# Deformable convolution after attention on one core: three of nine taps sampled densely instead of two

## The reference

```python
offset_feat = conv2d(concat([feat_l, feat_up * 2]), W_off, pad=0)          # 1x1
om = conv2d(offset_feat, W_om, pad=1) + b_om                              # 3x3 -> offsets and mask
feat_align = relu(deform_conv_v2(feat_up, offset, sigmoid(mask), W_dcn, b_dcn))
return feat_align + feat_l
```

## Time and profile before

| | before |
|---|---|
| median of 3 runs | 12687.91 us (12680.93 to 12688.98) |
| the profiled execution's own time | 12682.99 us |
| its span, first to last instruction | 12681.2 us |
| PE busy / weight loads | 9257.2 us (73%) / 5057.7 us (40%) |
| DVE busy | 7291.4 us (57%) |
| ACT busy | 4747.5 us (37%) |
| POOL busy | 10320.1 us (81%) |
| mean granted TensorE clock | 0.838 |

### The profile page before, as it was taken

The page is one execution under the profiler, slowest core; times in us unless marked ns, Lnnn a source line. Parts: engine busy times, 40 slices in busy tenths (PEclk is TensorE's granted clock), DMA queues, the critical chain, the costliest instruction groups (busy, mean ns, idle before and its releaser), DMA issues. The chain is left out here.

```text
span 12681.2 us, 168047 instructions
## 1 busy us (share of the span) xinstructions
PE 9257.2 (73%) x56052; PEld 5057.7 (40%) x56052; DVE 7291.4 (57%) x10291; ACT 4747.5 (37%) x6104; POOL 10320.1 (81%) x21509
## 2 busy tenths in 40 slices
PE   4677778775778777776577777777577777777754
PEld 1244444442444444443244344444234444444444
DVE  4356566644666666664566666665456666666443
ACT  1344444432434434433244344343233434334322
POOL 0278888885788888888488888888858888888888
PEclk7888888886888888888788888888788888888876
DMA  1222211110011111111011111111101111111100
GB/s 48 77 67 70 66 23 24 24 24 23 21 33 25 24 24 25 25 24 29 13 25 33 24 24 25 25 23 24 28 16 31 25 25 25 25 23 24 24 22 21
DMA packets 373774, 373.51 MB, mean 29 GB/s; under 512 B 129440, under 2 KB 219936, under 8 KB 372768
## 3 DMA queue, kind: packets, MB, share of 16 engines
q0 software_dynamic: 229376, 235.34, 8.9%
q10 hardware_dynamic: 97920, 71.35, 1.8%
q1 hardware_dynamic: 45472, 54.53, 1.6%
HBM read 316.66 MB, written 44.04 MB: 28 GB/s over the span
## 5 line engine op out<-in xcount | busy, mean ns | idle before, releaser
L469 POOL DMA_INDIRECT g<-patches,idx x7168 | 7156.6, 998 | 1112.4 <-issue 949.5
L905 DVE TENSOR_REDUCE mx<-ring 128x2 f32<-128x1024 f32 x2048 | 2411.1, 1220 | 2919.3 <-PE ring L666 2381.8
L541 ACT ACTIVATE p<-ring 128x1024 f32<-128x1024 f32 x2048 | 1984.8, 1021 | 3832.3 <-PE ring L724 2960.3
L465 POOL TENSOR_TENSOR carrier<-carrier 128x1 f32<-128x1 f32 x13824 | 3063.5, 250 | 122.0
L708 PE MATMUL ps_x<-fx,hats 128*128 128x208 f32 x12288 | 2520.1, 356 | 120.4 <-DVE hats L1048 78.8
L721 PE MATMUL ring<-qf,kf 32*128 32x512 f32 x8192 | 1459.9, 786 | 1515.3 <-ACT hats L551 816.3
L708 PEld LDWEIGHTS ps_x<-fx,hats 128*128 128x128 f32 x12288 | 2192.2, 196 | 671.2 <-issue 598.1
L734 PE MATMUL ps_a<-p,v 128*64 128x512 f32 x4096 | 1442.3, 790 | 39.0 <-DVE shared L932 37.6
L734 PE MATMUL ps_b<-p,v 128*64 128x512 f32 x4096 | 1247.2, 692 | 0.0
L1067 DVE TENSOR_TENSOR ps_x<-ps_x,chosen 128x416 f32<-128x416 f32 x1024 | 611.1, 597 | 1053.2 <-PE ps_x L708 844.1
L574 ACT COPY vt<-ps_x 128x256 f32<-128x256 f32 (+1 forms) x512 | 204.5, 399 | 2659.1 <-PE ps_x L780 1505.9
(11 more groups left out here) (125 smaller groups left out, 7601.4 us busy)
## 6 DMA issues: line engine op xcount, KB each, us to landing
g<-patches,idx POOLq DMA_INDIRECT x7168
patch_in<-in_fpad ACTq DMA_DIRECT2D x544, 64.0 KB
patches<-patch_out ACTq DMA_DIRECT2D x136, 256.0 KB
fx<-in_fpad SPq DMA_DIRECT2D x20, 416.0 KB
p<-in_x SPq DMA_DIRECT2D x4, 2048.0 KB
xq<-in_x SPq DMA_DIRECT2D x32, 256.0 KB
fs_s<-in_fs SPq DMA_DIRECT2D x32, 256.0 KB
xs<-in_x SPq DMA_DIRECT2D x32, 256.0 KB
```

Source lines behind the costliest of these rows:

```text
L465: last = nc.gpsimd.tensor_tensor(carrier[:, col:col + 1], carrier[:, 0:1], carrier[:, 0:1], ALU.add)
L469: nc.gpsimd.indirect_dma_start(out=g[:, j, :], out_offset=None, in_=patches[b], in_offset=bass.IndirectOffsetOnAxis(ap=idx[:, t, j:j + 1], ...
L541: nc.scalar.activation(p[:, (2 * kt + pair) % 4, :, :], ring[slot][:, :, :], ACT.Exp, scale=SCALE)\
L905: V.tensor_reduce(mx[:, n:n + 2, c], ring[slot][:, :, :], AX.X, ALU.max).then_inc(ring_free[slot], 1)
```

## The change

`DENSE` goes from 2 to 3 and `PICKED` from 7 to 6. Everything else follows from that or makes it fit:

- a tile has 48 indirect gathers instead of 56, in parts of 2, 2, 1 and 1 taps instead of 2, 2, 2 and 1;
- a tile has 6 sets instead of 4, which begin at key tiles 0, 1, 2, 4, 5, 6 of its eight; where one set's half 1 and the next set's half 0 fall on the same key tile, half 1 comes first;
- `hats` has three buffers instead of two, and ACT cuts the hats straight after the distances, in the same key tile;
- dense tap 0 is turned with part 2 and dense taps 1 and 2 with part 3; `vt` is ordered by these slots, and `align` goes through them by a table.

```diff
-DENSE = 2
+DENSE = 3
 PICKED = TAPS - DENSE
 PARTS = 4
 CUTS = tuple(min(2 * part, PICKED - (PARTS - part)) for part in range(PARTS + 1))
-LAST_TAPS = CUTS[PARTS] - CUTS[PARTS - 1] + DENSE
+DENSE_CUTS = (0, 0, 0, 1, DENSE)
+WIDTHS = tuple(CUTS[part + 1] - CUTS[part] + DENSE_CUTS[part + 1] - DENSE_CUTS[part] for part in range(PARTS))
+SLOTS = tuple(sum(WIDTHS[:part]) for part in range(PARTS))
+SLOT_TAPS = tuple(tap for part in range(PARTS) for tap in (*range(CUTS[part], CUTS[part + 1]),
+                                                           *range(PICKED + DENSE_CUTS[part], PICKED + DENSE_CUTS[part + 1])))
+HATS = 3
...
-        hats = sb("hats", [128, 2, 1 + PAIRS, SET_GROUPS * 128])
+        hats = sb("hats", [128, HATS, 1 + PAIRS, SET_GROUPS * 128])
...
-            return tuple((r, t, i, half) for half in range(2) for r, t, i in sets_with(s, kt, half))
+            return tuple((r, t, i, half) for half in (1, 0) for r, t, i in sets_with(s, kt, half))
...
-                made = hats[:, i % 2, :, :]
+                made = hats[:, i % HATS, :, :]
...
-                    for r, t, i in weighed_at(s, kt):
-                        cut_hats(uses, t, i)
                     for r, t in aligned_at(s, kt):
                         finish_tile(tile_number(r, t))
...
                     for r, t, i in hats_at(s, kt):
                         distances_to_hats(uses, t, i)
+                        cut_hats(uses, t, i)
...
-                for tap in range(TAPS):
-                    last = mm(aligned, wdcn_s[:, tap, :], vt[:, tap, :], start=tap == 0, stop=tap == TAPS - 1)
+                for k, tap in enumerate(SLOT_TAPS):
+                    last = mm(aligned, wdcn_s[:, tap, :], vt[:, k, :], start=k == 0, stop=k == TAPS - 1)
...
-                if part == PARTS - 1:
-                    for d in range(DENSE):
-                        last = tr(turned[:, (picked + d) * 128:(picked + d + 1) * 128], dval[:, t % 2, d * C:(d + 1) * C],
-                                  ident_s[:, :])
+                for k, d in enumerate(range(DENSE_CUTS[part], DENSE_CUTS[part + 1]), picked):
+                    last = tr(turned[:, k * 128:(k + 1) * 128], dval[:, t % 2, d * C:(d + 1) * C], ident_s[:, :])
```

More of the change, by code:

```diff
@@ L325, in build @@
         assert all(slots_in(o) % 2 == 0 for o in (FIRST, MID, LAST))
-        assert MID[-1][0] == "rows" and MID[0][0] == ("scores", 0)
+        assert ("rows", 2) in MID and MID[0] == (("scores", 0), 2)
         BATCH_SLOTS = USES_KV + slots_in(FIRST) + (STEPS_B - 2) * slots_in(MID) + slots_in(LAST)
@@ L571, in keep_turned @@
                 m = part_number(r, t, part)
-                width = 128 * (LAST_TAPS if part == PARTS - 1 else CUTS[part + 1] - CUTS[part])
+                width = WIDTHS[part] * 128
                 act.wait_ge(val_turned, m + 1)
-                nc.scalar.copy(vt[:, CUTS[part]:CUTS[part] + width // 128, :].rearrange("p k n -> p (k n)"), turned[:, 0:width]).then_inc(vt_ready, 1)
+                nc.scalar.copy(vt[:, SLOTS[part]:SLOTS[part] + WIDTHS[part], :].rearrange("p k n -> p (k n)"), turned[:, 0:width]).then_inc(vt_ready, 1)
             def step(s, b, i):
@@ L707, in blocks_of_half @@
                     for pair in range(PAIRS):
-                        last = mm(cells, hats[:, i % 2, 1 + pair, j * 128:(j + 1) * 128], fx[:, pair, :, group * GC:(group + 1) * GC],
+                        last = mm(cells, hats[:, i % HATS, 1 + pair, j * 128:(j + 1) * 128], fx[:, pair, :, group * GC:(group + 1) * GC],
                                   start=pair == 0, stop=pair == PAIRS - 1)
```

## The result

The changed kernel takes 14784.01 us (median; 14776.14 to 14813.88), the kernel before beside it 12684.42 us. The ratio is 1.166, 95% interval 1.164 to 1.168: slower by a sixth. I had forecast 15290 us, a fifth slower; the measured time lies within the range, 14600 to 16000. The profiled execution has a span of 14775.8 us.

A forecast was written before the change was run, and what follows sets the result against it. POOL was taken as the bound, PE's loop close behind; middle steps of 350.3 + 105 us added dense work (39 + 34 + 28 + 5, less 1), summed with start, image-boundary steps and tail, gave about 15290 us, range 14600 to 16000.

The forecast's parts named there:

- the bound and its thinness: Middle steps: POOL never stops at 360.2 us a step, with PE's loop close behind at about 350.
- my signs: Expected: POOL waiting over 100 us a step for `val`, PE waiting at halves but not for `val`, middle steps 455 us.
- the distances: Eight added sets a step, each 1.23 us of PE's time plus 2.3 of waiting for ACT: 28 us.
- halves and their wait: Sixteen added halves a middle step on PE: 39 us of work plus 34 us of waiting for DVE.
- the new wait: PE waits for `half_used` between a key tile's two halves: 8 x 1.6 + 8 x 2.6 = 34 us a step.
- the floor: Middle step's period with POOL taken away, set by the loop of PE, ACT and DVE: about 350 us.
- a mean outside 0.83 to 0.90: PE's mean granted clock in middle steps, 0.87 before; leaving this range would show the prediction wrong.
- The case of a rising clock: Rival: added work fills idle time, PE's time at 1.2 GHz goes, at most 47 us a step; 13920 us, chance 0.2.
- the cut ahead of the exponentials: ACT comes 0.6 us late to the exponentials in 24 key tiles: 5 us a step, bounds 0 and 14.
- its check on the distances: Start: second step 332 against 375 and 379 us, 43 for two tiles; own terms give 28 for distances, 15 for others.
- The tail: End of the run, set by POOL: from 554 us to 430, bounds 385 and 554.
- The faster rival: Rival: PE has room, added work vanishes in its idle time and only POOL's time counts; 12120 us, chance 0.03.

The follow-up runs named there:

- experiment 1: Kernel before, without the seventh gathered tap's 8 gathers a tile (patches stay zero): 12012.03 us, ratio 0.948.
- experiment 5: Changed kernel with 8 more gathers a tile into a tile that nothing reads: 14871.48 us, ratio 1.173.
- experiment 4: Changed kernel with the halves of sets 1 and 4 left out on PE and DVE, their distances, hats and weighing kept: 12915.01 us, ratio 1.019.
- experiment 3: Changed kernel with the hats cut one key tile later, behind the exponentials, except at the last key tile: 14747.52 us, ratio 1.163.
- experiment 9: Kernel before with PE's half put behind the distances in key tiles that have distances: 12659.97 us, ratio 0.9975.
- experiment 2: Changed kernel with two dense taps and two hat buffers, so only the new order remains: 12722.02 us, ratio 1.004.
- experiment 10: Kernel before with PE's half behind the distances and one small POOL addition ahead of each gather instead of two: 12047.67 us, ratio 0.949.
- experiment 11: Kernel before with half behind distances, one POOL addition ahead of each gather, and the seventh tap's 8 gathers a tile left out: 14837.21 us, ratio 1.170.
- experiment 12: Kernel before, old order, with the seventh tap's 8 gathers a tile left out and one POOL addition ahead of each gather: 14503.09 us, ratio 1.141.
- experiment 6: Changed kernel without DVE's multiplication in every half: 14415.56 us, ratio 1.137.
- experiment 7: Changed kernel with PE's aligning, turning and distances moved between a key tile's first and second half: 13812.82 us, ratio 1.089.

## Why the prediction came out so

**Right: the bound and its thinness.** POOL was the bound and PE's loop stood right behind it (experiments 1 and 5). Of the 51 us that POOL saves a middle step, I gave the kernel 10. Without the added dense work it is 18. Of my signs, POOL's wait came as 127 us a step, but only half of it is for `val` and the rest for `idx`, which I had not named; PE's wait for `val` is gone, and DVE waits longer for PE at its maxima (413 us in four steps; before it was 299 and another 70 put down to issue).

**Right: the distances.** Experiment 4 against 1 holds the distances, the cut and the gathered tap that is no longer weighed: forecast 28 + 5 - 1 = 32 us a middle step, measured 28.4. PE's wait for ACT, the larger part of the distances, is (225.3 - 148.5) / 4 = 19 us a step more, where 8 x 2.3 = 18 was forecast.

**Right in kind, 10 us too large: halves and their wait.** Forecast 39 + 34, measured 62.6. The direct part holds: 16 x 2.47 = 39. The term that was mis-sized is the new wait. I took 1.6 us behind a normal key tile and 2.6 behind a sampling; the 64 waits are 1.6 us each on average, 25.6 a step. By place in the trace they are 1.4 us at key tiles 1 and 2, 1.6 at 5 and 2.0 at 6, so behind a sampling (2 and 6) 1.7 and not 2.6. That fits DVE being hardly late once PE itself is later by the added half, more than I allowed.

**Mis-sized: the floor.** I put PE's loop at 350 by taking away only PE's waits for `val`. It is 342.6, because PE's own instructions took less time at the higher clock. My sum left the clock's share as it was, and I had named a mean outside 0.83 to 0.90 as a sign of being wrong; it went from 0.87 to 0.91, in experiment 1 as in the changed kernel. The Trainium skill (TensorE: Matmul & The Clock Gate, What's actually happening) says that activity releases the throttle. Experiment 1 agrees with it, where PE's busy share of four steps rose from 78% to 79%. The changed kernel doesn't follow from it, since that share fell to 74% and the clock rose as much. The case of a rising clock, 13920 us, supposed that all of the time at 1.2 GHz would go, 45 us a step. The granted clock says that most of it stays, 9% short of the full clock where it was 13%. PE's busy time fell by (1127.6 - 1072.3) / 4 = 14 us a step in experiment 1, and the floor by 8.

**Wrong in its parts: the cut ahead of the exponentials.** I charged 5 us to every step. In a middle step it is a gain of 3.4 us, and in the third and fourth steps, which also build tables, a loss of 47 and 41 (experiment 3). I had read the start for its check on the distances and not asked what else stood in ACT's queue there: the copies behind which the exponentials come even later.

Per middle step that is 8 for the floor, 10 for the halves with their wait and 4 for distances and cut together, 22 of 455. If the cut alone is 8 too high, as experiment 3 has it, the distances are about 5 too low. Over the run the distance of 509 us in the span (15285 against 14776) is made of 21 middle steps, -455, last ones -122, first ones -56, third and fourth +50, second +16, tail +57. The total is closer than its parts by luck: the start and the tail were too low by 124 us and hide a part of the 633 by which the other steps were too high. In the last steps experiment 4 has 319.9 where my terms give 300 + 32, so the base or the distances were too high by 12, and the halves are 54.6 and not 73.

**The tail** is POOL's, as forecast; POOL works 392 of 487 us in it. I counted five tiles and the trace has 768 / 144 = 5.3, and the rest beside them is 75 us and not 45.

**The faster rival** rested on weight loads at 40%. They went to 43% while PE's loop took the whole step: by the measurement, LDWEIGHTS busy time (the Trainium skill, Perfetto Trace Analysis, Identifying the Most-Contended Engine) doesn't tell how much an engine can take on when its idle time is made of waits within a loop.

**What stays open:** why the clock rose in experiments 1 and 9 and in the changed kernel; what the dense tap's earlier turning costs, which was only run under POOL's cover (experiment 2); what would shorten the loop of PE and DVE at 344 us in experiment 10; and what the stalls of experiments 11 and 12 are.

## What to carry to other kernels

Before work is moved off the busiest engine, ask for how long the next one waits for it: here 10 us a step, and 51 us of relief earned 18 (the waits and a higher clock) and cost 91. Work added to an engine that goes in order is only free where that engine would wait anyway. Put a buffer's second use right behind its first, and the reader's time is added in full (experiment 6). Put other work between, and a part of it is hidden: the wait at the halves fell by half, and with the shorter wait for ACT the run by 970 us (experiment 7). And weigh the cheaper way to relieve an engine first, its cost per piece, though experiment 12 says to test it at other loads.

## What the runs showed of the hardware

- *Spacing whose worth turns with the number of gathers.* With 56 gathers a tile, one addition ahead of each gather gave 12114 us; with 48, two gave 12012, and one gave 14503, though POOL had the least to do. In that kernel a gather is not slower (971 ns against 1011 in experiment 1), and the gathers' packets kept the DMA engines busy no longer (6.6% of 14500 us against 8.2% of 11993); DVE, ACT and then PE stall instead. The cause was not found.
- *The mean clock doesn't follow the length of the waits alone.* With the same instructions PE was busy 1127.6 us in four steps of the kernel before, at a granted clock of 0.87, and 1072.3 in experiment 1, at 0.91. But with PE's order alone changed, in steps of the same length and with more waiting for `val`, it was 1104.1 us at 0.90 (experiment 9).
- *Reading one PSUM buffer between two uses of it.* PE stood idle for 1.40 us between two halves, while DVE read the first with instructions of 0.60 and 0.59 us; without the multiplication the 64 waits of four steps fell from 102.2 to 49.8 us (experiment 6).
